# Fusion convolution by four row products: a deformable convolution layer on one core

## What is computed

```python
out_normal = _conv(x, w_normal)
offset = jnp.concatenate([_conv(x, w_offx), _conv(x, w_offy)], axis=1)
out_x = _deform_conv(x, offset, w_dx)      # 9 taps, each sampled bilinearly at its own offset
out_y = _deform_conv(x, offset, w_dy)
out = _conv(jnp.concatenate([out_normal, out_x, out_y], axis=1), w_fusion)   # 384 -> 128, 3x3
out = jax.nn.relu(_bn(out, bn1_g, bn1_b, bn1_m, bn1_v))
out = _bn(_conv(out, w_conv2), bn2_g, bn2_b, bn2_m, bn2_v)
return jax.nn.relu(out + x)
```

## Time and profile before

| what | value |
|---|---|
| median of 3 runs | 2706.34 us (2705.74 to 2707.16) |
| profiled execution, its own time | 2707.24 us |
| its span, first to last instruction | 2705.3 us |
| mean granted clock of TensorE | 0.989 |
| busy: PE, DVE, ACT, POOL | 2607.9, 1859.5, 1531.8, 1912.4 us |
| matmul instructions | 17840 recorded |
| gathers on POOL | 1800 |

### The profile page before, as it was taken

How to read it: one execution, slowest core, us unless ns; L and a number is a source line. 1 busy time by engine, 2 the same in 40 slices (tenths; PEclk the granted TensorE clock), 3 DMA queues, 4 the chain that set the end, 5 groups by cost and what they waited for, 6 DMA issues and landing times.

```text
span 2705.3 us, 49885 instructions
## 1 busy us (share of the span) xinstructions
PE 2607.9 (96%) x17840; PEld 2599.0 (96%) x17840; DVE 1859.5 (69%) x4967; ACT 1531.8 (57%) x3575; POOL 1912.4 (71%) x1806
## 2 busy tenths in 40 slices
PE   3679999999999999999999999999999999999999
PEld 3669999999999999999999999999999999999999
DVE  5767777776677777777767777776766676777730
ACT  5778777777555555555555555555555555555531
POOL 6777777777777777777777777777777777777720
PEclk9789999999999999999999999999999999999999
DMA  6767777777777777777777777766666666666620
GB/s 190 237 219 225 240 237 225 222 223 224 226 221 224 226 229 227 235 224 228 224 221 225 226 223 230 228 200 196 201 201 201 202 200 200 202 206 192 198 76 20
DMA packets 170167, 565.06 MB, mean 209 GB/s; under 512 B 31808, under 2 KB 31936, under 8 KB 169536
## 3 DMA queue, kind: packets, MB, share of 16 engines
q0 software_dynamic: 144000, 471.97, 58.8%
q1 hardware_dynamic: 25920, 89.91, 9.3%
HBM read 527.41 MB, written 34.34 MB: 208 GB/s over the span
## 4 chain that ended last, share of the span: by engine, by line
PE 92%; DVE 3%; ACT 2%; DMA 2%; POOL 1%; issue 1%; ACTq 0%; POOLq 0%; DVEq 0%
PE work L363 20%; PE work L369 20%; PE work L366 20%; PE acc L366 7%; PE acc L363 7%; PE acc L369 7%; PE turned L395 7%; PE work L348 4%; DMA cells<-in_xpair,index 1%; POOL cells L322 1%; DVE mixed L710 1%; PE work L355 1%; ACT mixed L495 1%; ACT samp L495 1%; DVE samp L716 0%
## 5 line engine op out<-in xcount | busy, mean ns | idle before, releaser
L322 POOL DMA_INDIRECT cells<-slope_table,index x1350 | 1422.4, 1054 | 513.2 <-issue 235.7
L495 ACT ACTIVATE samp<-mixed,wgt 128x128 f32<-128x128 f32 x1800 | 663.9, 400 | 309.7 <-DVE mixed L710 301.1
L363 PE MATMUL work<-feat,w_hi 128*128 128x320 f32 x2160 | 690.7, 320 | 2.4 <-ACT off_c L494 2.4
L369 PE MATMUL work<-feat,w_lo 128*128 128x320 f32 x2160 | 675.4, 313 | 0.0
L366 PE MATMUL work<-feat,w_hi 128*128 128x320 f32 x2160 | 675.0, 312 | 0.0
L322 POOL DMA_INDIRECT cells<-in_xpair,index x450 | 478.6, 1064 | 162.8 <-issue 79.0
L710 DVE SCALAR_TENSOR_TENSOR mixed<-cells,wgt 128x256 f32<-128x256 f32 x1350 | 557.0, 478 | 1.0
L716 DVE SCALAR_TENSOR_TENSOR samp<-mixed,wgt,samp 128x128 f32<-128x128 f32 x1800 | 509.1, 345 | 35.2 <-ACT samp L495 35.2
L662 DVE TENSOR_TENSOR samp_lo<-turned,samp_hi 128x640 fp32r<-128x640 f32 x360 | 295.2, 820 | 320.8 <-ACT samp_hi L494 320.5
L363 PE MATMUL acc<-samp_hi,w_hi 128*128 128x320 f32 x1440 | 449.5, 312 | 0.0
L366 PE MATMUL acc<-samp_lo,w_hi 128*128 128x320 f32 x1440 | 447.9, 311 | 0.0
(11 more groups left out here) (73 smaller groups left out, 3593.2 us busy)
## 6 DMA issues: line engine op xcount, KB each, us to landing
cells<-slope_table,index POOLq DMA_INDIRECT x1350, 3.7
slope<-in_xpair SPq DMA_DIRECT2D x27, 768.0 KB
slope_table<-slope SPq DMA_DIRECT2D x27, 768.0 KB, 4.5
x_raw<-in_xflat SPq DMA_DIRECT2D x40, 410.0 KB, 4.1
late<-in_x SPq DMA_DIRECT2D x40, 320.0 KB, 7.7
out<-late SPq DMA_DIRECT2D x40, 320.0 KB, 3.7
cells<-in_xpair,index POOLq DMA_INDIRECT x450, 3.8
late<-in_weights SPq DMA_DIRECT2D x3, 1152.0 KB, 6.6
```

The source lines that it names most:

```text
L322: eng.indirect_dma_start(out=cells[:, g, :], out_offset=None, in_=cell_rows, in_offset=bass.IndirectOffsetOnAxis(ap=index[:, par, j, k:k + ...
L363: ins = eng.matmul(dst, taps_hi[:, w], hi, start=start, stop=False, skip_group_check=True)
L369: return eng.matmul(dst, w_lo[:, w], hi, start=False, stop=stop, skip_group_check=True)
L495: return eng.activation(dst, src, ACT.Copy, scale=scale)
```

## The change

The fusion convolution is taken over pairs of output rows: of four input rows r0 to r3 it uses r0-r2, r1+r2, r2-r1 and r1-r3 with four transformed sets of weights, and the two output rows are sums and differences of the four products. Each of the three column taps and three maps needs four products of 4x80 pixels for 8 rows, so F has 4 x 9 = 36 groups of three in place of 54.

- ACT copies the maps as float32 into `raw` and no longer splits them. In tap 6 DVE combines rows of `raw` into `d_raw` (`rows_combined`), ACT rounds them to `d_hi`, DVE makes `d_lo` (`rows_low`). The last row waits for the next strip (`last_row`, taps 1 and 2), with two rows kept in `keep`. The row copies above and below `feat` go away.
- The output is gathered from four banks in turn: one ACT instruction and four of DVE (two after the second product), then relu by ACT and the low part by DVE over all 8 rows.
- The weights are transformed on chip by four DVE instructions (`weights_form`), now 72 tiles; `w_lo` shares its memory with the raw weights. All weight loads are issued at the start.
- The slope table is made in 54 pieces of half the size; `dynamic_dma_scratch_size` goes from 8192 to 4096; `SLICES` is written anew.

```diff
-    [("C", 0, 0, 9), ("C", 1, 0, 2)],
-    [("C", 1, 2, 9), ("O", 0, 0, 3)],
-    [("O", 1, 0, 3), ("F", 0, 0, 8)],
...
+    [("F", 2, 6, 9), ("F", 3, 0, 6)],
+    [("F", 3, 6, 9), ("N", 0, 0, 5)],
+    [("N", 0, 5, 9), ("N", 1, 0, 4)],
+    [("N", 1, 4, 9)],
...
+            def rows_combined(s):
+
+                at_least(eng, n_out, 2 * s + 2)
+                at_least(eng, acc_out, 4 * s + 4)
+                even, odd = (raw[:, :, :, :].rearrange("p g (i z) w -> p g i z w", z=2)[:, :, :, z, :] for z in range(2))
+                to = d_raw[:, :, :, 1:1 + W]
+                eng.tensor_tensor(to[:, :, SUM_ROW:SUM_ROW + PAIRS, :], even, odd, ALU.add).then_inc(sums_done, 1)
+                eng.tensor_tensor(to[:, :, DIFF_ROW:D_ROWS, :], odd, even, ALU.subtract).then_inc(sums_done, 1)
+                eng.tensor_tensor(to[:, :, 1:Z_ROWS - 1, :], raw[:, :, 0:ROWS - 2, :], raw[:, :, 2:ROWS, :], ALU.subtract)\
+                    .then_inc(zs_done, 1)
+                if s % STRIPS:
+                    at_least(eng, keep_done, s)
+                    ins = eng.tensor_tensor(to[:, :, 0, :], keep[:, :, 1, :], raw[:, :, 1, :], ALU.subtract)
...
+            def rows_low(s):
+
+                at_least(eng, sums_hi, s + 1)
+                low(d_lo[:, :, SUM_ROW:D_ROWS, 1:1 + W], d_raw[:, :, SUM_ROW:D_ROWS, 1:1 + W], d_hi[:, :, SUM_ROW:D_ROWS, 1:1 + W]).then_inc(sums_lo, 1)
+                at_least(eng, zs_hi, s + 1)
+                low(d_lo[:, :, 0:Z_ROWS - 1, 1:1 + W], d_raw[:, :, 0:Z_ROWS - 1, 1:1 + W], d_hi[:, :, 0:Z_ROWS - 1, 1:1 + W]).then_inc(zs_lo, 1)
...
+                        if job == "F" and q == T - 1:
+                            if fl.fuse:
+                                at_least(eng, f_done, T * s + 4)
+                                eng.scalar_tensor_tensor(out=mid_odd, in0=bank_rows, scalar=minus1[:], in1=mid_odd,
+                                                         op0=ALU.mult, op1=ALU.add).then_inc(f_four, 1)
+                            if fl.rows:
+                                rows_combined(i - 1)
...
+                            if fl.rows:
+                                rows_low(i - 1)
...
-                if fl.strip:
-                    for d in range(2):
-                        for half in range(2):
-                            rows = slice(1 + half * HR, 1 + half * HR + HR)
-                            at_least(eng, acc_hi_done, 4 * i + 2 * d + half + 1)
-                            low(feat[:, par, 3 + 2 * d, rows, 1:1 + W],
-                                acc[2 * d + half][:, 0:HALF].rearrange("p (r w) -> p r w", w=W),
-                                feat[:, par, 2 + 2 * d, rows, 1:1 + W]).then_inc(acc_lo_done, 1)
```

## The result

The changed kernel took 2829.99 us, median of 4 runs (2821.60 to 2838.04), against 2706.04 for the kernel before on the same chip: a ratio of 1.0457, 95% interval 1.0419 to 1.0495. It is slower by 124 us. The forecast was 2693.4, and the time lies outside the stated range, 2570 to 2790. The profiled execution took 2821.6 us with a span of 2819.8.

A forecast was written before the change was run, and what follows sets the result against it. PE bounds the kernel before; POOL's gathers were to take over. First gather 20, gathers 2415.6, block 163.8, weights 3, tail 90: 2692.4, plus 1.9 less 0.9, gives 2693.4 us; range 2570 to 2790.

The forecast's parts named there:

- PE's price: F on PE loses 18 of 54 groups per strip, 2160 matmuls at 0.15 us: 8.1 us less per step.
- The price of each DVE instruction of the block: DVE's new tap 6 combinations and low parts, each priced from element count at 1.045 ns: 9.2 us in a row.
- Ordinary gathers: POOL's gathers outside the block: 1.342 us each with the 0.30 gap, against 1.25 undisturbed; 2415.6 us for 1800.
- the 3 put down for the weights: Weight transform and larger weight series in steps 0 to 2: 6 us of two-input DVE work, half lost to POOL.
- The block: DVE's two-SBUF-input instructions in tap 6 delay POOL's gathers by 4.2 us per step, 163.8 us over 39 steps.
- The rule of the next end: A gather blocked by a two-input DVE instruction gets its turn when that instruction ends: about 4.35 us lost per step.
- if it is held through a whole series: Alternative for tap 6: a gather waits until DVE's whole series ends, losing 8.1 us per step; not taken.
- The tail: Time after the last gather, through its block, deformed tap, remaining F groups and the end: 90 us.
- The start: Time until POOL's first gather: about 20 us, as the first weights copied are smaller.
- PE and DVE alone: Step length if POOL did not bind, including PE's stall before tap 8: 60.3 us.
- The wait before tap 8: PE stalls before tap 8 because DVE's tap 6 block delays the samples: 3.7 to 4.1 us per step.
- The second rival: POOL slower: gathers held through the series (2840 us) or ordinary ones costing 1.40 (2797); halfway 2755 us; chance 20%.

The follow-up runs named there:

- a_free_split: Changed kernel with one SBUF input for nearly all two-input DVE instructions, combined rows' low parts moved to taps 7 and 8, part of computation omitted: 2464 us.
- a_one: Changed kernel, the tap 6 block's row combinations and low parts replaced by one-SBUF-input instructions of equal element count, part of computation omitted: 2660 us.
- b_long: Kernel before with halved DMA scratch plus fourteen one-SBUF-input DVE instructions of 880 elements (13.7 us) in tap 6 of steps 1 to 40: 2989 us.
- a_tiny: Changed kernel with DVE's tap 6 block and ACT's two roundings cut to four columns of few rows, part of computation omitted: 2570 us.
- a_blk: Changed kernel with one SBUF input for mixed, samp, low parts of x and mid, and slopes; block keeps two; part of computation omitted: 2588 us.
- a_free: Changed kernel with one SBUF input for nearly every DVE instruction that had two, inside and outside the block, part of computation omitted: 2582 us.
- a_gap: Changed kernel plus eight short one-SBUF-input DVE instructions of 64 elements before, between and after the block's instructions, nothing left out: 2748 us.
- a_early_gap: Changed kernel with sums combined earlier, after F's second product, plus eight short one-SBUF-input DVE instructions, nothing left out: 2751 us.
- b_one: Kernel before with halved DMA scratch plus nine one-SBUF-input DVE instructions of 880 elements (8.8 us) in tap 6: 2755 us.

## Why the prediction failed, step by step

**Right.** PE's price: 2160 matmuls fewer; a_free_split shows 6.1 us of the gain of 8.1 per step once POOL and the block are out of the way. The price of each DVE instruction of the block: 1.07, 1.06, 1.57, 0.32, 0.74 and, for the two low parts, 3.88 us, against 1.07, 1.07, 1.57, 0.32, 0.80 and 3.91. That POOL takes over as the bound and gives the gain back, at a gap of 0.30 throughout; that nothing is lost by the scratch (shown on the kernel before).

**Wrong in size, all on POOL.** The sum had a span of 2692.4, measured were 2819.8, 127 us more:

- *Ordinary gathers*, taken at 1.342 with their gap: the 1685 that meet no block took 1.082 + 0.304 = 1.386. That is 0.044 x 1800 = 79, less the 3 put down for the weights: 76 us. The step that failed is "I take 239.66/230 + 0.30 = 1.342": the mean of one stage of the kernel before, where 29 of 230 gathers waited, was taken for a kernel in which none waits. The other end of my own bounds, 1.40 from the early stage, the only one in which POOL sets the pace, was nearer. The same ordinary two-input work cost 0.11 us per gather in the kernel before and 0.14 to 0.15 in a_one and b_long: the mean of one kernel does not carry over. Why it is dearer here stays open; that POOL never waits is not enough, since in a_tiny it never waits either and the mean is 1.061.
- *The block*, 4.2 us per step: measured 5.1 above an ordinary gather (115 gathers in 40 blocks at 2.863 us, 5.5 above an undisturbed one), 41 us more. The rule of the next end was right for most blocks, and in a_blk for all (4.0 us). The step that failed is "if it is held through a whole series": it was set against the other as one of two laws, while both occur, the hold to the end in 15 of 40 blocks. The argument against it, that nine series per step at 3.3 us would have cost 24 us, excludes only that it happens every time.
- *The tail*: 103.5 us behind the last gather against 90, 13.5 more. Two blocks without POOL beside them hold PE, and from 2755 to 2775 us, around the second one, PE is busy for 12.7 of 20 us at a granted clock of 0.74.
- *The start*: first gather at 17.4 in place of 20, 2.6 less. Together 76 + 41 + 13.5 - 2.6 = 128, for the 127 to explain.

**PE and DVE alone**: 60.3 us per step were forecast; a_free shows 61.4, and 0.7 more for the real `mixed` and `samp`. The wait before tap 8 was there (3.47 us in most of a_free's steps, 4.06 in the row of the changed kernel above, 3.7 to 4.1 forecast), the lower clock behind it was missing from the sum. It did not decide here.

**The chances.** The second rival had this result in its range, 2755 to 2840, by both of its mechanisms in part: 41 of the 146 us of the one and 79 of the 104 of the other. 20% was too little: it needed only 0.5 us per step more than my sum, the loss of the block was taken at the lower of two values, and the ordinary gather below the mean of all.

The Trainium skill (SBUF — State Buffer, section "Who interferes with whom") says that a DVE instruction with at most one SBUF input does not contend with GpSimd, and that where two do contend, the second to come is blocked until the first ends. a_free agrees with the one (mean gather 0.947 us) and a_blk, in every block, with the other (no gather over 2.83 us); the 8.75 us across seven instructions go beyond it.

## What to carry to other kernels

Where an engine's instructions have a fixed gap, compare its idle time with count times gap: equal means that it is the bound, whatever its busy share says. Price contention by the stage in which the contended engine sets the pace, and take a hold through a whole series as a case that occurs in part of the steps. Where DVE must run two-input instructions back to back beside gathers, a tiny one-input instruction between them (0.13 us each) can pay (82 us in a_gap) or not (a_early_gap); look for what it does to the series next to it.

## What the runs showed that was not expected

- A hold seems to depend on hundredths of a microsecond, and on more. Of the gathers of the changed kernel near the first two combinations, those that start 0.06 to 0.43 us after the start of one all get in at its end (12), while 6 of the 7 that start within 0.03 us of it are held for 7.5 to 8.6 us more, and of 17 that start 0.74 to 0.81 us after the start of the first 9 are held for 7.8 to 7.9 and 2 for 3.1, these in blocks with L842. Of a_blk's gathers nine start in that last stretch too, and all get in at the next end. What distinguishes the held from the others is open. Since the steps then differ (62 to 73 us in one run, from the second image on), the time of such a kernel varies more: its four runs span 16 us, those of a_free 1 us.
- More work on DVE made the kernel 82 us faster (a_gap).
- Waits of PE of 4.06 and 5.4 us are followed by some 3.5 to 5 us at a granted clock of 0.50, while b_one, whose steady step is 0.8 us longer than that of the earlier trace rows, stays at 1.00 from 1355 to 2000 us.
